# Products of a constant tile on TensorE in five places of the first batch where it waits

## What the reference computes

```
x  = x + conv_attention(ln_c(x))     # deformable attention
t  = tokens of x                     # 3136 tokens of 96 channels
t  = t + moe(ln_t(t))                # 4 experts, 96 -> 384 -> 96, exact gelu, top 2 gates
```

## Time and profile before

| what | us |
|---|---|
| median of 3 runs | 752.38 |
| the three runs | 751.11, 752.38, 756.92 |
| the profiled execution: span from first to last instruction | 749.4 |
| TensorE busy in it | 707.8 (94%) |
| VectorE, ScalarE, GpSimd busy | 582.8, 384.5, 216.9 |

### The profile page before, as it was taken

How to read it: one execution, slowest core, us unless ns; L and a number is a source line. 1 busy time by engine, 2 the same in 40 slices (tenths; PEclk the granted TensorE clock), 3 DMA queues, 4 the chain that set the end, 5 groups by cost and what they waited for, 6 DMA issues and landing times.

```text
span 749.4 us, 9619 instructions
## 1 busy us (share of the span) xinstructions
PE 707.8 (94%) x3186; PEld 495.8 (66%) x3186; DVE 582.8 (78%) x1511; ACT 384.5 (51%) x722; POOL 216.9 (29%) x184
## 2 busy tenths in 40 slices
PE   5798999799999999999999999999998999999996
PEld 5556566566676666556767566666664665788884
DVE  4889648899999858699999477899975275677774
ACT  2314124744464614744556218545542256899995
POOL 4001700012128610111168201222285121344443
PEclk9998999799999999999999999999999999999999
DMA  8007200044464530345654422435645201121111
GB/s 195 9 0 198 53 9 1 7 98 86 89 185 115 98 56 10 68 103 119 155 129 83 86 48 46 82 80 101 190 102 109 35 20 49 47 69 51 66 47 37
DMA packets 29697, 58.66 MB, mean 78 GB/s; under 512 B 6224, under 2 KB 20176, under 8 KB 29360
## 3 DMA queue, kind: packets, MB, share of 16 engines
q0 software_dynamic: 11584, 17.90, 15.4%
q1 hardware_dynamic: 14336, 32.59, 14.7%
q10 hardware_dynamic: 3728, 7.55, 3.3%
HBM read 30.30 MB, written 14.65 MB: 60 GB/s over the span
## 4 chain that ended last, share of the span: by engine, by line
PE 56%; DVE 19%; DMA 7%; ACT 6%; POOL 5%; issue 5%; POOLq 0%; ACTq 0%
PE py L746 9%; PE pd L662 8%; PE ph L578 7%; DVE val L1133 6%; POOL big L1469 4%; DMA xbuf<-ye 4%; DVE query L1133 3%; PE pa L650 3%; PE pa L529 2%; PE ph L762 2%; PE ph L782 2%; PE ph L784 2%; PE ph L763 2%; PE ph L783 2%; PE ph L764 2%
## 5 line engine op out<-in xcount | busy, mean ns | idle before, releaser
L746 PE MATMUL py<-hid,w 128*96 128x448 f32 x504 | 234.4, 546 | 11.5 <-ACT hid L1006 8.7
L1006 ACT ACTIVATE hid<-ph,b 128x448 f32<-128x448 f32 x252 | 158.9, 632 | 148.1 <-PE ph L764 144.8
L762 PE MATMUL ph<-x_hi,w_hi 96*128 96x448 f32 x252 | 164.4, 653 | 0.0
L1480 POOL DMA_DIRECT2D xbuf<-ye x76 | 66.6, 877 | 327.2 <-DMA xbuf<-ye 163.2
L1469 POOL DMA_INDIRECT big<-value_table,rows x64 | 87.8, 1372 | 90.5 <-DVE rows L1193 56.5
L746 PEld LDWEIGHTS py<-hid,w 128*96 128x96 f32 x504 | 81.6, 165 | 31.2 <-ACT hid L1006 12.6
L763 PE MATMUL ph<-x_lo,w_hi 96*128 96x448 f32 x252 | 93.5, 371 | 0.0
L764 PE MATMUL ph<-x_hi,w_lo 96*128 96x448 f32 x252 | 92.8, 368 | 0.0
L1482 POOL TENSOR_TENSOR xbuf<-xbuf,ye 96x448 f32<-96x448 f32 x36 | 53.9, 1497 | 102.6 <-DVE ye L1416 99.9
L1416 DVE SCALAR_TENSOR_TENSOR ye<-py,b,gate_all 96x448 f32<-96x448 f32 x112 | 75.3, 674 | 9.3 <-PE py L746 7.3
L1443 DVE TENSOR_TENSOR hid_lo<-hid,hid_hi 128x448 fp32r<-128x448 f32 x84 | 59.7, 710 | 27.3 <-ACT hid L1015 27.1
(11 more groups left out here) (165 smaller groups left out, 1081.2 us busy)
## 6 DMA issues: line engine op xcount, KB each, us to landing
gate_all<-gate_rows SPq DMA_DIRECT2D x56, 336.0 KB, 3.5
xbuf<-ye POOLq DMA_DIRECT2D x76, 168.0 KB, 3.4
value_table<-valT ACTq DMA_DIRECT2D x6, 1176.0 KB, 8.9
out<-xbuf SPq DMA_DIRECT2D x28, 168.0 KB, 2.0
xbuf<-in_x SPq DMA_DIRECT2D x3, 1176.0 KB, 10.1
value_table<-valT SPq DMA_DIRECT2D x2, 672.0 KB, 5.3
big<-value_table,rows POOLq DMA_INDIRECT x64, 2.8
value_table<-valT SPq DMA_DIRECT2D x2, 504.0 KB, 5.0
```

Of the source, the lines that this page charges most:

```text
L746: nc.tensor.matmul(py[e % 2][0:C, 0:GPIX], w2[:, c, :], hid[:, k % 3, :], start=(j == 0), stop=(j == CPE - 1)).then_inc(hid_used, 1)
L762: nc.tensor.matmul(bank, w1_hi[:, cols], xh(b, g), start=True, stop=False)
L1006: nc.scalar.activation(hid[:, k % 3, :], ph[k % 2][:, 0:GPIX], ACT.Gelu, bias=b1[:, k % NCH:k % NCH + 1]).then_inc(hid_act, 1)
L1480: pool.dma_start(to, ye[0:C, e, :], accum_op=ALU.add).then_inc(ye_summed, 16)
```

## The change

A tile `warm` (a view of `hid[:, 2, 0:224]`) is set to 1.0 by VectorE as its first instruction, and a helper `keep_busy(n)` multiplies its first 128 columns (stationary) with all 224 (moving), in float32 with 128 rows, n times into `py[1]`. The results aren't read. Thirty-two such products are put on TensorE, in five places that are waits in the kernel before: 6 ahead of everything, 14 between `x_to_tokens(0)` and `quarters_back(0)`, 4 behind `off_to_channels(0)`, 4 behind `quarters_back(1)`, and 4 behind group 1 of `x1_back(0)`. Nothing is removed and nothing else is moved. TensorE waits for `warm_ready` first.

```
+WARM = 224
+        warm = hid[:, 2, 0:WARM]
+        warm_ready = sem("warm_ready")
+            def keep_busy(number):
+                for k in range(number):
+                    nc.tensor.matmul(py[1][:, 0:WARM], warm[:, 0:128], warm, start=True, stop=True)
...
             def head(b):
                 pe.wait_ge(tiles_zero, 1)
                 x_to_tokens(b)
+                keep_busy(14)
                 quarters_back(b)
...
                     transposes(bank, [x1T[:, GRP * g + k, 0:C] for k in range(GRP)], TP, C).then_inc(dve_full, 1)
+                    if first(b) and g == 1:
+                        keep_busy(4)
                     if g == GATES_AFTER:
...
                 off_to_channels(b)
+                keep_busy(4)
                 values_to_tokens(b, slots=range(VALUE_HALF, QT))
...
                 quarters_back(b + 1)
+                keep_busy(4)
                 x1_back(b, plan, chunks_to)
...
+            pe.wait_ge(warm_ready, 1)
+            keep_busy(6)
             pe.wait_ge(ident_in, 16)
             head(0)
...
+            nc.vector.memset(warm, 1.0).then_inc(warm_ready, 1)
             nc.vector.memset(first_tiles[:, :, QUARTERS, :], 0.0)
```

## The result

The changed kernel takes 746.78 us in the median of 15 runs (742.84 to 755.02), the kernel before, on the same chip, 753.63 (748.82 to 761.09). The ratio is 0.992, with a 95% interval of 0.9894 to 0.9946: some 6 us less, where 9.8 were forecast. The sign is right, the size too large by two thirds. The time lies inside the range of eight in ten (737.5 to 749.5), but not inside the forecast's own (738 to 744.9). A ratio leaves out runs more than 1.5% above the fastest, so it can differ from that of the medians.

What follows compares the result with a forecast made beforehand. TensorE's order and clock in the first 160 us bound the kernel; 4.8, 0.9, 1.0, 3.2 and 0 us, plus overlap in `key_values`, gave 9.8 us, hence 742.5 us; eight in ten: 737.5 to 749.5.

Steps and rivals of the forecast that it cites:

- The sum: Two chains meeting at `key_values`, its last quarter ending at 94.0 instead of 103.8 us: gain 9.8 us.
- R1: Rival: the clock rises too late for `x_to_tokens`, only in the fourteen products; gain 6.2, 746 us, chance 0.18.
- R2: Rival: head won, but pauses between token transposes from 57 us let the clock fall; 746 us, chance 0.12.
- What bounds the kernel: TensorE's order in the first 160 us and its clock; batch 0's gain by 160 us reaches the end one for one.
- The six: Ahead of everything: they raise the clock, centring products take 5.8 instead of 10.74 us; 4.8 us gained, VectorE included.
- The fourteen: Before `quarters_back(0)`: faster copies (1.75 us) and convolutions (1.9), half of each taken: 0.9 all engines, 1.0 TensorE alone.
- The middle: Four products behind `off_to_channels` hold the clock; offsets 0.9, centring 1.6, convolutions 0.7: 3.2 us for TensorE alone.
- The end: The two fours at 133 and 135 us: the clock falls in the next hole instead; 0 us, bounds -0.8 and +1.9.
- The overlap in `key_values`: Its first three quarters (3.9 us) run while the last is sampled, so it no longer runs in one block.
- R3: Rival, slower: the products don't raise the clock; the fourteen add 4.2 us, the four 0.9; 757.5 us, chance 0.07.
- R4: Rival: little effect in the end, falls landing otherwise or later batches taking the gain back; 750 to 753, chance 0.10.
- Transposes: From 23 to 29.5 us the clock doesn't rise in transposes, but at 131 to 132 us transposes alone held it.

Runs made afterwards that it cites:

- `cover_late`: The changed kernel with the remaining holes filled by more products and GpSimd's last diagonal build held back until VectorE has split the weights: 741.89 us, ratio 0.9868.
- `cover_trim`: `cover_late` without its five products around the offset products (three before, two behind): 741.72 us, ratio 0.9856 to the kernel before.

## Why the prediction was right, and where its size was off

The sum had the right mechanism, idle products that raise or hold the clock in a bare chain, and terms of the wrong size. That the time fell inside the range of eight in ten is in part luck: 746 stood in the prediction as the value of R1 and of R2, and it came out so for another reason, a clock lost before `quarters_back`.

**What bounds the kernel**: right. In `cover_late` the gates come 12.4 us before the mean of before, and 7 to 13 us arrive in the time. From the gates to the end the traces differ among themselves, 600.9 to 607.5 us over all kernels, without order; that is part of the noise on every comparison here. The clock has a part in it: it falls once more for some 4 us in the first trace of before (at 623.9 us) and in those of the changed kernel (at 575.7; at 553.9 and 622.1; at 569.6).

**The six, 4.8 us for all engines**: the products were right (5.88, 5.99 and 6.09 us in three traces, for 5.8), the conclusion "the statistics and VectorE after them included" was not. 1.5 to 2.1 us of it go to the collision with GpSimd. The prediction asked who else is queued behind, and not what a faster chain would run into beside it. By the run and the trace without the six, they are worth 0 to 2 us.

**The fourteen, 0.9 and 1.0 us, half of each**: too high. In all three traces the clock was lost around 20 us: nothing of the copies' 1.75 us is left, and the convolutions' 27 products took 21.10, 20.44 and 18.05 us, where before they took 19.57 and 20.57. The holes that the prediction named did it, and the collision was a part of why the first of them was 2.4 to 3.0 us long instead of 1. With more products in both holes (three traces) the clock held. Sum of these two steps: the convolutions started 3.4, 3.5 and 2.6 us earlier, where 5.7 were forecast, and the fourth half block of them 3.3 earlier in the mean of the traces, where 6.7 were. These are the steps that failed: the 4.8 us of the six taken whole for VectorE, and half of each term of the fourteen. They account for most of the missing 4 us. With holes and collision removed the start moved by 6.9 and 6.1, and the times came to 0.987 and 0.986.

**The middle, 3.2 us**: right in its mechanism. Offset products 1.47 us in all three traces, clock held in two of three. In the third R2 happened: the gates came 3.7 and 4.8 us later than in the other two, of which 0.7 and 2.2 were there already at the fourth convolution (48.39 against 47.69 and 46.19). That leaves 2.6 to 3.0 us for R2, a little less than was written. The run with only the six and the fourteen prices the whole at some 4 us by the ratios. The expectation of that run had doubted this term; the doubt was wrong.

**The end, 0 us**: right. The fall moved from 135.7 to 138.8, and taking both fours out changed nothing that the runs can tell. Only with the hole before the first second product filled does the end give something: from that product to the gates 2.2 us (134.64 to 136.83) instead of 3.9.

**The overlap in `key_values`**: right in two of three traces.

**R1** can be held against the trace without the six, which is its case. It had the fourteen end near 24.5 us; its own terms give 23.5 (3.2 us at 1.2 GHz hold 4.3 of them, the other 9.7 take 3.7 us), and the trace has 23.3. The price was wrong as well: by the ratios the six are worth less than its 3.6 us. **R3**, slower, wasn't seen: with the six, the centring products took 5.88 to 6.41 us in all ten traces. **R4** wasn't seen as a whole either: the falls did land otherwise, but nothing of the gain was lost behind the gates (603.2 us from there to the end in the mean of before, 603.5 after).

**Transposes** hold a clock that is up, as the prediction had it: with the holes filled, `quarters_back` ran at 2.4 GHz. The other half doesn't hold. That the clock doesn't rise in them the prediction had from the trace of before and from the Trainium skill, "TensorE: Matmul & The Clock Gate", Part 4. In two traces here it rose after 6.4 us of transposes alone (at 26.7 and 26.2 us), and the measurement decides.

## What to carry to other kernels

A wait filled with idle products pays as far as the clock then holds. Here the four behind `off_to_channels` paid by themselves (some 4 us), because what follows has no long wait; the six and the fourteen, with two holes open behind them, brought the start of the convolutions little more than half of what was forecast, and all of it once the holes were filled and the late build was out of the way. Before a chain is moved forward, look at what runs beside its new place on the engines that it doesn't wait for. And where the clock decides, one trace isn't the kernel: take several, and compare a mark at the end of the changed stretch.

## What the runs showed that was not expected

One program loses the clock in different places from execution to execution. The changed kernel's 15 executions span 742.84 to 755.02 us, with a mean granted clock of 0.990 to 0.974 in the records; its quickest (742.84 and 742.96) had 0.989 and 0.990, its slowest 0.974.

The clock also fell while TensorE was busy, behind sixteen records of two moving columns each (63.7 us above, and 57.8 in `cover_trim`). In nine other traces it held there; what decides isn't shown.

The clock rose in transposes alone in two traces, and in the same transposes of other executions it didn't.

A VectorE instruction with two inputs waited for the end of a GpSimd instruction, 1.74 to 2.15 us instead of 0.20, in all seven traces that had the six and the builds in their old place.
